# Graph layers on one core: weights with the input channel innermost, vector products in one instruction, sums added one by one, the span test once per layer

## What is computed

```python
# layer 0: features of the neighbours, scaled by degree, summed per node
norm = deg_inv_sqrt[row] * deg_inv_sqrt[col]
x = layernorm(x + segment_sum(x[row] * norm[:, None], col))
# layer 1: a message per edge, with weights made from the edge's own 32 features
h = relu(edge_feat @ W1 + b1)                    # 64 per edge
w = (h @ W2 + b2).reshape(e, 4, 8, 8)            # four 8x8 matrices per edge (i, o)
m0 = ALPHA * (einsum('ei,eio->eo', s_e * sh0, w_000) + C110 * einsum('eim,em,eio->eo', v_e, sh1, w_110))
m1 = ALPHA * (einsum('ei,em,eio->eom', s_e, sh1, w_011) + einsum('eim,eio->eom', v_e * sh0, w_101))
x = layernorm(x + segment_sum([m0, m1], dst) + self-interaction(x))
```

## Time and profile before

| | |
|---|---|
| median of 3 runs | 5685.9 us (5684.65 to 5692.03) |
| profiled execution, first to last instruction | 5691.5 us |
| VectorE busy | 3000.7 us, 53% |
| POOL busy | 3201.0 us, 56% |
| TensorE busy | 2619.5 us, 46% |
| ScalarE busy | 325.3 us, 6% |
| mean granted TensorE clock | 0.697 of full speed |

### The profile page before, as it was taken

The page is one execution under the profiler, slowest core; times in us unless marked ns, Lnnn a source line. Parts: engine busy times, 40 slices in busy tenths (PEclk is TensorE's granted clock), DMA queues, the critical chain, the costliest instruction groups (busy, mean ns, idle before and its releaser), DMA issues. The chain is left out here.

```text
span 5691.5 us, 47787 instructions
## 1 busy us (share of the span) xinstructions
PE 2619.5 (46%) x12834; PEld 1908.4 (34%) x12834; DVE 3000.7 (53%) x4177; ACT 325.3 (6%) x556; POOL 3201.0 (56%) x3341
## 2 busy tenths in 40 slices
PE   8981111111111111111257666666666666666662
PEld 8981111111111111111234444444444444444441
DVE  5561000000000100000169999999999999999994
ACT  0000000000000000000011111111111111111110
POOL 0006666666666666666455555656565656555550
PEclk9997555555555555555567787878787878778785
DMA  0000000000000000000011111111111111111110
GB/s 21 0 11 12 12 12 12 12 12 12 12 12 12 12 12 12 12 12 12 13 25 23 23 21 23 21 23 21 23 21 23 21 23 21 23 21 23 21 22 12
DMA packets 169134, 95.17 MB, mean 17 GB/s; under 512 B 100154, under 2 KB 153915, under 8 KB 168920
## 3 DMA queue, kind: packets, MB, share of 16 engines
q0 software_dynamic: 106496, 54.74, 6.6%
q1 hardware_dynamic: 62620, 40.21, 2.6%
HBM read 89.90 MB, written 4.81 MB: 17 GB/s over the span
## 5 line engine op out<-in xcount | busy, mean ns | idle before, releaser
L282 POOL DMA_INDIRECT xg<-x_table,idx x1664 | 1570.2, 944 | 1156.2 <-DVE feat L695 602.5
L282 POOL DMA_INDIRECT xg<-scaled_x_table,idx x1664 | 1625.8, 977 | 771.8 <-issue 579.1
L572 DVE TENSOR_TENSOR sumT<-sumT,ps 32x64 f32 x832 | 172.6, 207 | 2281.6 <-remote 1876.9
L383 PE MATMUL ps<-oh,xg 128*32 128x64 f32 x3328 | 378.0, 310 | 2029.5 <-DMA xg<-scaled_x_table,idx 2016.8
L452 PE MATMUL ps<-w,hT 128*128 128x256 f32 x3328 | 979.4, 445 | 482.9 <-DVE prod L711 428.4
L720 DVE TENSOR_REDUCE red<-prod 128x192 f32<-128x1536 f32 x416 | 1201.0, 2905 | 0.0
L383 PEld LDWEIGHTS ps<-oh,xg 128*32 128x32 f32 x3328 | 347.8, 172 | 2059.8 <-issue 2059.2
L452 PEld LDWEIGHTS ps<-w,hT 128*128 128x128 f32 x3328 | 688.6, 218 | 971.3 <-DVE prod L711 715.8
L383 PE MATMUL ps<-oh,msg 128*32 128x64 f32 x3328 | 370.1, 310 | 398.9 <-DVE msg L732 388.0
L383 PEld LDWEIGHTS ps<-oh,msg 128*32 128x32 f32 x3328 | 347.3, 172 | 467.4 <-issue 467.4
L445 PE MATMUL ps<-efT,w 128*64 128x512 f32 x832 | 490.9, 674 | 5.1 <-ACT x_sb L318 5.1
(11 more groups left out here) (71 smaller groups left out, 598.1 us busy)
## 6 DMA issues: line engine op xcount, KB each, us to landing
xg<-scaled_x_table,idx POOLq DMA_INDIRECT x1664
efT<-in_efT SPq DMA_DIRECT2D x104, 256.0 KB, 2.5
xg<-x_table,idx POOLq DMA_INDIRECT x1664
idx<-in_src SPq DMA_DIRECT2D x208, 8.0 KB
sh<-in_sh SPq DMA_DIRECT2D x104, 32.0 KB, 2.3
x_sb<-in_x SPq DMA_DIRECT2D x1, 1568.0 KB
scaled_x_table<-z_sb SPq DMA_DIRECT2D x1, 1568.0 KB
x_table<-q_sb SPq DMA_DIRECT2D x8, 196.0 KB
```

Source lines behind the costliest of these rows:

```text
L282: pool.indirect_dma_start(xg[k][:, t, :], None, table, bass.IndirectOffsetOnAxis(ap=idx[k][:, t:t + 1], axis=0),).then_inc(s_g[layer][GPC ...
L383: mm = pe.matmul(ps_sum[:, k, j, :], rows[:, TPG * j + t, :], oh[k][:, TPG * j + t, :], start=(t == 0), stop=(t == TPG - 1))
L572: dve.tensor_tensor(sumT[:, bass.ds(base, WIN)], sumT[:, bass.ds(base, WIN)], ps_sum[:, k, j, :], ALU.add).then_inc(s_acc[layer], 1)
```

## The change

Four edits, and the loops around them:

- the weight table is copied once into `w2t`, turned so that the input channel i is innermost; products stand as (matrix, o, i), and the addends of the reduction are neighbours
- `vec` is written as (m, i), and the three products with its components are one instruction that reads the fourth matrix three times
- the four additions of the chunk before no longer stand together: one follows each reduction
- the test of `all_near` stands once around each layer's loop, on both engines, with a loop for the near and a loop for the wide case.

```diff
+        w2t = sb("w2t", [P, 4, MUL, MUL])
-        vec = sb("vec", [P, TPC, 3 * MUL])
+        vec = sb("vec", [P, TPC, 3, MUL])
...
+            def gathered_sums(sums):
                 for k in range(2):
-                    window_sums(0, xg[k], 2 * i + k, k, 16 * TPG * i + 16 * TPG, False)
+                    sums(0, xg[k], k, k, 16 * TPG, True)
+                with pe.Fori(1, PAIRS) as i:
+                    for k in range(2):
+                        sums(0, xg[k], 2 * i + k, k, 16 * TPG * i + 16 * TPG, False)
+
+            with pe.If(all_near == 1):
+                gathered_sums(window_sums)
+            with pe.Else():
+                gathered_sums(wide_sums)
...
                 if not first:
-                    pe.wait_ge(s_prod, 4 * (g - 1))
+                    pe.wait_ge(s_prod, 2 * (g - 1))
                 for t in range(TPG):
-                    mm = pe.matmul(ps_w[j % 2][:, t, :], hT[j % 2][:, t * P:(t + 1) * P], w2[:],
+                    mm = pe.matmul(ps_w[j % 2][:, t, :], hT[j % 2][:, t * P:(t + 1) * P],
+                                   w2t[:].rearrange("p c o i -> p (c o i)"),
...
+            dve.wait_ge(s_w2x, 3)
+            dve.tensor_copy(w2t[:].rearrange("p c o i -> p c i o"),
+                            w2[:].rearrange("p (c i o) -> p c i o", c=4, i=MUL)).then_inc(s_w2x, 1)
...
-            def add_sums(layer, n, k):
-
-                with dve.If(all_near == 1):
-                    dve.wait_ge(s_sum[layer], n + 1)
-                    for j in range(GPC):
+            def add_sums(layer, n, k, groups=range(GPC)):
+
+                dve.wait_ge(s_sum[layer], n + 1)
+                for j in groups:
...
-                dve.tensor_tensor(vec[:], xg[k][:, :, MUL:D], sh0.to_broadcast([P, TPC, 3 * MUL]),
-                                  ALU.mult).then_inc(s_ft, 1)
+                dve.tensor_tensor(vec[:].rearrange("p t m i -> p t i m"),
+                                  xg[k][:, :, MUL:D].rearrange("p t (i m) -> p t i m", m=3),
+                                  sh0.unsqueeze(2).to_broadcast([P, TPC, MUL, 3]), ALU.mult).then_inc(s_ft, 1)
...
                 dve.tensor_tensor(
-                    prod[b][:, :, 0:3].rearrange("p t c i o -> p t (c i) o"),
-                    ps_w[b][:, :, 0:3 * MUL * MUL].rearrange("p t (c o) -> p t c o", o=MUL),
-                    feat[k][:, cut, :].unsqueeze(3).to_broadcast([P, TPG, 3 * MUL, MUL]),
+                    prod[b][:, :, 0:3],
+                    ps_w[b][:, :, 0:3 * MUL * MUL].rearrange("p t (c o i) -> p t c o i", c=3, o=MUL),
+                    feat[k][:, cut, :].rearrange("p t (c i) -> p t c i", c=3).unsqueeze(3)
+                    .to_broadcast([P, TPG, 3, MUL, MUL]),
                     ALU.mult).then_inc(s_prod, 1)
-                for m in range(3):
-                    dve.tensor_tensor(
-                        prod[b][:, :, 3 + m],
-                        ps_w[b][:, :, 3 * MUL * MUL:].rearrange("p t (i o) -> p t i o", o=MUL),
-                        vec[:, cut, m::3].unsqueeze(3).to_broadcast([P, TPG, MUL, MUL]),
-                        ALU.mult).then_inc(s_prod, 1)
+                dve.tensor_tensor(
+                    prod[b][:, :, 3:6],
+                    ps_w[b][:, :, 3 * MUL * MUL:].rearrange("p t (o i) -> p t o i", o=MUL).unsqueeze(2)
+                    .to_broadcast([P, TPG, 3, MUL, MUL]),
+                    vec[:, cut].unsqueeze(3).to_broadcast([P, TPG, 3, MUL, MUL]),
+                    ALU.mult).then_inc(s_prod, 1)
...
                 dve.tensor_reduce(
-                    red[:, TPG * j:TPG * (j + 1)].rearrange("p t c o -> p (t c) o"),
-                    prod[j % 2][:].rearrange("p t c i o -> p (t c) o i"),
+                    red[:, TPG * j:TPG * (j + 1)].rearrange("p t c o -> p (t c o)"),
+                    prod[j % 2][:].rearrange("p t c o i -> p (t c o) i"),
...
                 for j in range(GPC):
                     products(n, k, j, first and k == 0 and j < 2)
                     if j >= 1:
                         reduce_products(n, j - 1)
-                    if j == 1 and not (first and k == 0):
-                        add_sums_general(1, n - 1, GPC * n + 1)
-                    if j == 2 and not (first and k == 0):
-                        add_sums(1, n - 1, 1 - k)
+                    if follows and near_sums and j >= 1:
+                        add_sums(1, n - 1, 1 - k, [j - 1])
...
                 reduce_products(n, GPC - 1)
+                if follows and near_sums:
+                    add_sums(1, n - 1, 1 - k, [GPC - 1])
                 messages(n, k)
...
+            with dve.If(all_near == 1):
+                edge_chunks(True)
+                add_sums(1, CHUNKS - 1, 1)
+            with dve.Else():
+                edge_chunks(False)
+                add_wide_sums(1, CHUNKS - 1, GPC * CHUNKS)
```

More of the change, by code:

```diff
@@ L386, in window_sums @@
[L386 to L396, removed]
+                pe.wait_ge(s_oh[layer], n + 1)
@@ new lines, in window_sums, with wide_sums @@
+                if not first:
+                    pe.wait_ge(s_acc[layer], GPC * (n - 1))
+                for j in range(GPC):
+                    for t in range(TPG):
+                        mm = pe.matmul(ps_sum[:, k, j, :], rows[:, TPG * j + t, :], oh[k][:, TPG * j + t, :],
+                                       start=(t == 0), stop=(t == TPG - 1))
+                mm.then_inc(s_sum[layer], 1)
+            def wide_sums(layer, rows, n, k, landed, first):
+                HALVES = TPC // 2
+                with pe.Fori(0, WIDES) as v:
+                    if landed is None:
+                        pe.wait_ge(s_msg, 3 * n + 3)
+                    else:
+                        for j in range(GPC):
+                            pe.wait_ge(s_g[0][GPC * k + j], landed)
+                    for m in range(HALVES):
+                        pe.wait_ge(s_woh[layer], n * (WIDES * HALVES) + v * HALVES + m + 1)
+                        for t in range(2):
+                            mm = pe.matmul(ps_wide, rows[:, 2 * m + t, :], wide_oh[:, t, :],
+                                           start=(m == 0 and t == 0), stop=(m == HALVES - 1 and t == 1))
+                        mm.then_inc(s_wmm[layer], 1)
+                pe.wait_ge(s_wmm[layer], (n + 1) * (WIDES * HALVES) + 1)
+                pe.sem_inc(s_sum[layer], 1)
@@ L464, in chunk, with message_sums @@
                     if j == 2 and not (first and k == 0):
[L465 to L469, removed]
+                        sums(1, msg[1 - k], n - 1, 1 - k, None, first)
+            def message_sums(sums):
                 for k in range(2):
-                    chunk(2 * i + k, k, 32 * i + 32, False)
-            weights(GPC * CHUNKS - 1, 1, False)
-            window_sums(1, msg[1], CHUNKS - 1, 1, None, False)
+                    chunk(k, k, 32, True, sums)
+                with pe.Fori(1, PAIRS) as i:
+                    for k in range(2):
+                        chunk(2 * i + k, k, 32 * i + 32, False, sums)
+                weights(GPC * CHUNKS - 1, 1, False)
+                sums(1, msg[1], CHUNKS - 1, 1, None, False)
+            with pe.If(all_near == 1):
+                message_sums(window_sums)
+            with pe.Else():
+                message_sums(wide_sums)
             sums_to_rows(1)
@@ L680, in features @@
                 if not first:
[L681 removed]
+                    dve.wait_ge(s_prod, 2 * GPC * n)
                 sh0 = sh[k][:, :, 0:1]
@@ L739, in edge_chunk @@
                 dve.wait_ge(s_scal, n + 1)
-                if not (first and k == 0):
+                if follows:
                     dve.wait_ge(s_msg, 3 * n)
```

126 lines of the change are left out of this document (59 added, 67 removed).

## The result

The changed kernel takes 6314.3 us (median of 4 runs, 6309.7 to 6316.3) beside 5685.3 us of the kernel before (4 runs): ratio 1.110, 95% interval 1.109 to 1.112. It is slower by 629 us where 513 us less were forecast. Of the rivals, E (6182 us, chance 0.13) is the one that names what happened; the measured time is 132 us above its own.

What follows compares the result with a forecast made beforehand. VectorE bounds the layer-1 edge stage at 25.73 us a chunk; after the change POOL would, at 20.8. The 4.93 us saved, times 104, is 513 us: 5685.9 becomes 5173 us, range 5120 to 5515.

Steps and rivals of the forecast that it cites:

- E: Layer-1 edge stage: late TensorE results are seen only when POOL pauses, two chunks take 61.0 us; 6182 us, chance 0.13.
- VectorE's terms: Layer-1 chunk on VectorE: reduction gains 4.61, products 0.48, additions 1.36, vec loses 0.15 us; 25.74 becomes 19.44.
- the +0.29 end of my bounds: Writing vec 8 floats apart in layer 1: +0.29 us a chunk at L720's slow pace, +0.15 taken.
- A: Layer-1 edge stage runs at POOL's pace, 20.8 us a chunk; 5173 us, chance 0.45.
- POOL as the floor: Layer-1 gathers: POOL's 16 instructions take 19.97 us a chunk, 20.8 with 0.5 and 0.35 for meeting VectorE.
- Rival C: Layer-1 edge stage: VectorE's messages, one-hot and features hold POOL, 22.25 us a chunk; 5324 us, chance 0.08.
- the overlap in the sum: Layer-1 chunk takes POOL's 20.8 us, with VectorE's 19.44 and TensorE's 17.3 beside it; gain 513 us.
- B: Layer 0's POOL stop also slows layer 1, 23.1 us a chunk; 5410 us, chance 0.22 including anything towards A.
- F: Layer 0: POOL's 5.69 us pause, 52 times, goes or doubles, moving the time 296 us either way; chance 0.05.

Runs made afterwards that it cites:

- e5: The changed kernel itself, on a chip where the kernel before takes 5692.3 us: 6331.0 us, ratio 1.113.
- e4: The kernel before with the turned order alone (w2 turned, reductions of neighbours, features written 8 apart), beside 5400.3 us: 4939.3 us, ratio 0.915.
- e9: The kernel before with the turned order alone, on a chip where the kernel before takes 5677.9 us: 6382.9 us, ratio 1.124.
- e7: The changed kernel, but each layer-1 gather waits until all transfers of the gather before it have landed, beside 5692.3 us: 5812.1 us.
- e10: The changed kernel without the turned order (w2 not turned, addends read 8 apart), beside 5677.9 us: 5629.7 us, ratio 0.991.
- e8: The changed kernel, but in layer 1 SP's index and edge-data transfers after the first two chunks are left out, beside 5677.9 us: 6317.7 us.
- e6: The changed kernel, but in layer 1 POOL keeps at most 8 transfers open, beside 5692.3 us: 6235.3 us, ratio 1.095.
- The half gather: The changed kernel, but POOL gathers only 8 of a chunk's 16 tiles in layer 1: 4706.8, 4707.6 and 4708.5 us.
- e14: The changed kernel without the turned order, on a chip where the kernel before takes 5401.1 us: 5192.7 us, ratio 0.961.
- e1: The changed kernel, but each layer-1 gather waits until all transfers of the gather before it have landed, beside 5400.3 us: 5078.0 us, ratio 0.940.
- e2: The changed kernel, but in layer 1 POOL keeps at most 8 transfers open, beside 5400.3 us: 4869.2 us.
- e3: The changed kernel, but in layer 1 SP's index and edge-data transfers after the first two chunks are left out, beside 5400.3 us: 4863.0 us.

## Why the prediction was wrong, point by point

- **VectorE's terms held.** Reduction 1740 ns for 1753. One product instruction of 947 ns. Additions at 199 to 204 ns with no 0.64 us gap in layer 1, as in A. `vec` came out at 837 ns, the +0.29 end of my bounds where I took +0.15: 0.14 us a chunk, under a cover that hid it. The Trainium skill (SBUF — State Buffer, "Door 1: The DMA port swizzle") says that each access that crosses to a new 16-byte line pays a penalty; it gives no size, but it pointed to the right end of my bounds, and the 837 ns agree.
- **POOL as the floor held, on the 5400 kind.** 20.5 us a chunk for the 20.8 of my sum: 0.40 us at the one-hot (1.34 for 0.94), 0.11 at the features (1.05), nothing to see elsewhere, where I took 0.5 and 0.35. Rival C (22.25) is refuted there; it counted L695 among the instructions with two inputs in SBUF, and its row has one. The saving of 529 us stands beside my 513. But the kernel before takes 5400 there, so this is not the case that was predicted, and its closeness doesn't redeem the forecast.
- **The step that failed: the overlap in the sum.** The sum put a chunk at POOL's 20.8 us, with VectorE's 19.44 and TensorE's 17.3 wholly beside them, and gave nothing for late results of TensorE, though E named them. On the 5686 kind a chunk takes 31.7 us: in every second chunk VectorE stands some 19 us for weights that TensorE has long made, because POOL no longer pauses between the two gathers, and TensorE itself falls to one instruction in about 2 us. The text set against E that "signals early in a run of POOL are prompt, and VectorE needs most of them early". That is true of the first half of the run, and irrelevant: one result late per cycle is enough, and after the change the second half of POOL's run lies under the next chunk's products. The earlier trace rows had ScalarE held for 14.47 us and the earlier trace rows VectorE for 37.76, and both went on only once POOL had paused. The sum needed just that pause of layer 1 to vanish, so its forecast was only good on the condition that E is wrong; I put it beside E instead.
- **E had the mechanism nearly right.** POOL runs 32 instructions, the weights of the second product are seen behind them, and two chunks make one cycle. It has results seen only when POOL pauses; the typical cycle also shows some seen inside the run, 12 and 16 us late.
- **E's price was low.** It gave 61.0 us for two chunks. The cycles of the changed kernel are 61.5 to 64.9, 64.2 in the mean. The terms, as medians: POOL's run is 40.9 us, not 39.9 (the meetings with VectorE, and in some runs a pause of 1.67 us); the longest wait ends 3.4 us behind it (5.1 in e5), not 3.0; and from there to POOL's next gather it is 20.4 us, not 18.1, since ScalarE, and behind it the weights of the third product, wait for a TensorE that is still catching up.
- **B and F** drew on the same stop in layer 0 as a thing of its own. It goes with E's behaviour: in every kernel that was profiled it is there on the 5686 kind and absent on the 5400 kind. F's "should the pause go" came with the chip, not with the loops: e4, which has the loops of before, is without it too. F's 296 us took 5.69 for all 52 stops, which add up to 262.
- **The dose**, on the 5686 kind, POOL's stop against the mean time of a chunk: none 32.3 us (e5), 0.6 us 32.5 (e9, 984 instructions in 2000 us), 2.3 us 26.9 (e7), 3.8 us 25.2 (e10), 6.1 us 25.7, with no cycle (before). These kernels differ in VectorE's pace too; only e5 with e7, and the stops inside e10, differ in the stop alone. Before, it was VectorE's slowness that gave POOL its stop.

What is shown, on the 5686 kind: that a stop of POOL put back takes away four fifths of the loss (e7 changes nothing else), that inside e10 the long waits go with the short stops, that the turned order alone brings the cycle (e9), and that neither SP's transfers (e8) nor more than 8 open transfers (e6) are needed. It is not that every stop will do: in e7 the long wait came back 28 times, though POOL had stopped for some 2.4 us one gather before. What is argued only: that the pace of TensorE and VectorE isn't a second condition. The half gather, which would have shown it, ran three times on the 5400 kind and never on the other. For it speaks layer 0, where TensorE is busy 385 of 2400 us and its sums are held all the same (this line is of the changed kernel's first profile):

```profile
1573.07 0.21 DVE L594 TENSOR_TENSOR sumT<-sumT,ps 32x64 f32 x1 [38.13 <-remote]
```

What makes one chip hold results and another not stays open; nothing in the profiles names it. The best version for both stays open as well: the kernel of e10 and e14 is faster than the one before on either kind (0.991 and 0.961), the changed kernel is better still on one (0.903) and worse on the other (1.113).

## What to carry to other kernels

When a rival says that a stall is what keeps something else in order, price the forecast on both sides of that stall before summing: the change that took away the last pause of a gathering POOL gained 529 us on one chip and cost 639 on another, by one behaviour that two idle rows ("remote", ended by POOL's pause) already showed. If a result of one engine is seen only when another pauses, leave the pause in, or measure the kernel with it put back (one wait, e7) before tuning anything else. And run the kernel before on each chip: without that, e1 to e4 would have been read as cures.

## What the runs showed of the hardware that I had not expected

- The same kernel takes 5397 to 5401 us on four chips and 5678 to 5692 on two; POOL's stops in layer 0, which come to 262 us, are in the traces of one kind and not of the other. A change of ratio 0.903 on a chip of the first kind is 1.113 on one of the second.
- On the 5686 kind, from about 17 us into a run of POOL's gathers, TensorE's instructions come mostly 1.4 to 2.8 us apart, and its results reach VectorE and ScalarE late: in the typical cycle by 12, 16 and 30 us, the last of them 3.4 us behind the run's end. On the 5400 kind ScalarE starts 0.04 us after the matmul, with POOL running through.
- A write of 384 floats with neighbours 8 floats apart takes 837 ns (L710), with neighbours side by side 551 (L686 before).
- POOL's gather instruction takes 1.3 to 1.5 us beside a one-hot of 1024 elements (up to 2.00 in the changed kernel's first trace) and 1.05 beside the features, 0.94 beside products out of PSUM. The Trainium skill (GPSIMD Engine Reference, "Key points") names instructions with two SBUF inputs as what disturbs GpSimd; these rows agree, and price it at 0.5 us in a chunk.
